# The first unit's matrix cut in halves, the second x loaded in two transfers, and one VectorE cut that reads SBUF: a batched matrix product with residual

## The reference

```python
def _L0_cond_ref(x, fwd_steps, T):
    Tb = T[fwd_steps - 1]
    return jnp.einsum('bij,bjk->bik', Tb, x)

def reference(x, itok_B_1_98, L0_cond_T):
    return x + _L0_cond_ref(x, itok_B_1_98, L0_cond_T)
```

## Time and profile before

| | before |
|---|---|
| median of 3 runs | 104.38 us (104.21 to 104.92) |
| the profiled execution's own time | 104.17 us |
| its span, first to last instruction | 102.4 us |
| TensorE busy | 95.8 us (94%) |
| VectorE busy | 86.9 us (85%) |
| GpSimd busy | 72.7 us (71%) |
| ScalarE busy | 66.0 us (64%) |
| mean rate of the transfers | 247 GB/s |

### The profile page before, as it was taken

The page is one execution under the profiler, slowest core; times in us unless marked ns, Lnnn a source line. Parts: engine busy times, 40 slices in busy tenths (PEclk is TensorE's granted clock), DMA queues, the critical chain, the costliest instruction groups (busy, mean ns, idle before and its releaser), DMA issues.

```text
span 102.4 us, 1799 instructions
## 1 busy us (share of the span) xinstructions
PE 95.8 (94%) x440; PEld 79.8 (78%) x440; DVE 86.9 (85%) x99; ACT 66.0 (64%) x86; POOL 72.7 (71%) x38
## 2 busy tenths in 40 slices
PE   4968999999999999999999999999999999999950
PEld 4957888868888888888888888888888888888840
DVE  0074798999999999999999999999999999993250
ACT  0765699659578685858585859587786858462100
POOL 2000548999989799897979797979798996918100
PEclk9999999999999999999999999999999999999999
DMA  1899999994899889897998489999899730405064
GB/s 48 299 223 407 343 219 214 378 310 125 355 319 293 273 261 326 273 315 207 353 336 274 98 284 352 294 349 255 266 304 323 226 147 19 189 3 205 0 276 134
DMA packets 20604, 25.28 MB, mean 247 GB/s; under 512 B 2290, under 2 KB 16882, under 8 KB 19698
## 3 DMA queue, kind: packets, MB, share of 16 engines
q10 hardware_dynamic: 3602, 15.34, 40.4%
q1 hardware_dynamic: 16992, 9.84, 36.7%
HBM read 16.78 MB, written 8.39 MB: 246 GB/s over the span
## 4 chain that ended last, share of the span: by engine, by line
PE 89%; DMA 5%; SPq 2%; DVE 0%; issue 0%
PE same L409 29%; PE same L420 28%; PE diff L431 28%; DMA T_sb<-T 5%; PE turned L397 2%; SPq L160 1%; PE same L388 1%; PE diff L441 1%; PE same L441 0%; SPq L146 0%; DVE out_sb L374 0%
## 5 line engine op out<-in xcount | busy, mean ns | idle before, releaser
L280 POOL TENSOR_TENSOR xL<-x_sb,xH 128x1024 fp32r<-128x1024 f32 x14 | 33.8, 2414 | 9.2 <-ACT xH L197 9.2
L293 POOL TENSOR_TENSOR TD_r<-TH_r,TL 128x1024 fp32r<-128x1024 f32 x14 | 33.8, 2415 | 2.5 <-issue 2.5
L409 PE MATMUL same<-xH,TH_r 128*128 128x512 f32 x128 | 34.5, 391 | 0.0
L420 PE MATMUL same<-xL,TL 128*128 128x512 f32 x128 | 34.4, 391 | 0.0
L431 PE MATMUL diff<-xD,TD_r 128*128 128x512 f32 x124 | 33.2, 390 | 0.1
L224 ACT ACTIVATE diff<-same 128x512 f32<-128x512 f32 x31 | 18.0, 582 | 22.2 <-PE same L420 22.2
L330 DVE STREAM_TRANSPOSE turned<-T_sb 128x512 f32<-128x512 f32 x28 | 29.1, 1085 | 0.0
L409 PEld LDWEIGHTS same<-xH,TH_r 128*128 128x128 f32 x128 | 23.9, 188 | 5.1 <-ACT TH_r L209 0.2
L420 PEld LDWEIGHTS same<-xL,TL 128*128 128x128 f32 x128 | 23.9, 188 | 4.9
L431 PEld LDWEIGHTS diff<-xD,TD_r 128*128 128x128 f32 x124 | 23.2, 188 | 5.3 <-issue 0.5
L350 DVE TENSOR_TENSOR out_sb<-x_sb,diff 128x512 f32<-128x512 f32 x31 | 21.0, 678 | 4.7 <-PE diff L431 4.7
(11 more groups left out here) (20 smaller groups left out, 18.7 us busy)
## 6 DMA issues: line engine op xcount, KB each, us to landing
out<-out_sb ACTq DMA_DIRECT2D x15, 512.0 KB, 5.1
T_sb<-T SPq DMA_DIRECT2D x112, 64.0 KB, 4.3
x_sb<-x ACTq DMA_DIRECT2D x6, 1024.0 KB, 6.3
x_sb<-x SPq DMA_DIRECT2D x1, 1024.0 KB, 10.0
x_sb<-x ACTq DMA_DIRECT2D x2, 256.0 KB, 3.7
x_sb<-x ACTq DMA_DIRECT2D x1, 512.0 KB, 4.6
T_sb<-T SPq DMA_DIRECT2D x2, 256.0 KB, 5.6
T_sb<-T SPq DMA_DIRECT2D x1, 512.0 KB, 6.8
```

Source lines behind the costliest of these rows:

```text
L280: nc.gpsimd.tensor_tensor(half(xL, h), x_sb[b % X_SLOTS][:, i:i + 2], half(xH, h).bitcast(fp32), ALU.subtract).then_inc(xL_ready, 2)
L293: nc.gpsimd.tensor_tensor(TD_r[s][:], TH_r[s][:].bitcast(fp32), TL[s][:].bitcast(fp32), ALU.subtract).then_inc(TD_ready, 2)
L409: nc.tensor.matmul(same[U % 2][:], TH_r[p][:, i, j], xH[s][:, j], start=(j == 0), stop=False)
L420: done = nc.tensor.matmul(same[U % 2][:], TL[p][:, i, j], xL[s][:, j], start=False, stop=(j == N - 1))
```

## The change

Unit 0 is turned into both banks of `turned`, two blocks in each, and TH(0) and TL(0) are made in two pieces of 256 columns, one for each bank; the first two matmuls of high(0) wait for the first piece alone. Because unit 0 now lies in both banks, turn(1) waits until TL(0) is made. The three matmuls of the unit matrix behind turn(0) go ahead of it (`WARM` 10 for 7 and 3). x of batch 1 comes in two transfers of 512 KB, each with a semaphore of its own, and `cut_x_half(2)` and `cut_x_half(3)` wait for one each. xD of half 1 reads xH in SBUF, and ScalarE's copy of half 1 is left out. GpSimd's TD(1) waits for that xD.

```diff
-    WARM, REWARM = 7, 3
+    WARM = 10
...
+        first_halves = [(turned[:, 0, 0:2], slice(0, 2)), (turned[:, 1, 2:4], slice(2, 4))]
...
             load_T(sp, t, 0)
-            load_x(sp, 1)
+            load_second_x(sp, 0)
+            load_second_x(sp, 1)
             sp.wait_ge(itok_loaded, 16)
...
             def cut_x_half(h):
                 b = h // 2
-                act.wait_ge(x_loaded[b % X_SLOTS], 16 * ((b - 1) // X_SLOTS + 1))
+                if b == 1:
+                    act.wait_ge(half_x_loaded[h % 2], 16)
+                else:
+                    act.wait_ge(x_loaded[b % X_SLOTS], 16 * ((b - 2) // X_SLOTS + 1))
...
+            def cut_first_T():
+                for i, ready in enumerate((first_half_TH_ready, TH_ready)):
+                    bank, blocks = first_halves[i]
+                    if i == 0:
+                        act.wait_ge(first_half_turned, 1)
+                    else:
+                        wait_turned(act, 1)
+                    nc.scalar.activation(TH_r[0][:, 0, blocks], bank, COPY, scale=LEAN / RADIX).then_inc(ready, 1)
...
-            cut_T(0)
+            cut_first_T()
             copy_xH_half(0)
             cut_T(1)
-            copy_xH_half(1)
             seed(0)
...
             def cut_T(U):
                 pool.wait_ge(TL_ready, U + 1)
+                if U == 1:
+
+                    pool.wait_ge(xD_ready, N)
...
-                dve.wait_ge(xH_copied, 2 * h + 2)
+
+                if h != 1:
+                    dve.wait_ge(xH_copied, max(h, 1))
...
+                high = half(xH, h).bitcast(fp32) if h == 1 else xH_copy[:]
+                nc.vector.scalar_tensor_tensor(half(xD, h), half(xL, h).bitcast(fp32), -RADIX, high,
                                                ALU.mult, ALU.add).then_inc(xD_ready, 2)
...
+            def cut_first_T():
+                for i, ready in enumerate((first_half_TH_ready, TH_ready)):
+                    bank, blocks = first_halves[i]
+                    dve.wait_ge(ready, 1)
+                    cut = nc.vector.scalar_tensor_tensor(TL[0][:, 0, blocks], TH_r[0][:, 0, blocks].bitcast(fp32), -RADIX,
+                                                         bank, ALU.mult, ALU.add)
+                cut.then_inc(TL_ready, 1)
...
+            def turn_first():
+                wait_T_loaded(pe, 0)
+                rows = T_sb[0][:, 0].rearrange("p (c j) -> p j c", j=N)
+                for j in range(N):
+                    done = nc.tensor.transpose(turned[:, j // 2, j], rows[:, j], eye[:])
+                    if j == 1:
+                        done.then_inc(first_half_turned, 1)
+                done.then_inc(turned_by_pe, 1)
...
             def turn(U):
                 s, n = U // N % T_SLOTS, U % N
                 wait_T_loaded(pe, U)
-                if U >= 2:
-                    pe.wait_ge(TL_ready, U - 1)
+                pe.wait_ge(TL_ready, max(U - 1, 1))
...
-                pe.wait_ge(TH_ready, U + 1)
                 for j in range(N):
+                    if U == 0 and j < 2:
+                        pe.wait_ge(first_half_TH_ready, 1)
+                    else:
+                        pe.wait_ge(TH_ready, U + 1)
...
             warm_up()
-            turn(0)
-            rewarm(REWARM)
+            turn_first()
             multiply_high(0)
```

More of the change, by code:

```diff
@@ L69, in cond_resid @@
         first_x_loaded = [sem(f"first_x_loaded{i}") for i in range(len(FIRST_X))]
+        half_x_loaded = [sem(f"half_x_loaded{i}") for i in range(2)]
         T_loaded = [[sem(f"T_loaded{s}_{n}") for n in range(N)] for s in range(T_SLOTS)]
@@ L72, in cond_resid @@
         turned_by_dve = sem("turned_by_dve")
+        first_half_turned = sem("first_half_turned")
+        first_half_TH_ready = sem("first_half_TH_ready")
         TH_ready = sem("TH_ready")
@@ L135, in half, with load_x, load_second_x @@
             return tiles[h // 2 % X_SETS][:, 2 * (h % 2):2 * (h % 2) + 2]
-        def load_x(eng, b, tiles=slice(0, N)):
-            eng.dma_start(x_sb[b % X_SLOTS][:, tiles], x_part[b, :, tiles]).then_inc(x_loaded[b % X_SLOTS], 16)
+        def load_x(eng, b):
+            eng.dma_start(x_sb[b % X_SLOTS][:], x_part[b]).then_inc(x_loaded[b % X_SLOTS], 16)
+        def load_second_x(eng, i):
+            eng.dma_start(x_sb[1][:, 2 * i:2 * i + 2], x_part[1, :, 2 * i:2 * i + 2]).then_inc(half_x_loaded[i], 16)
         def load_T(eng, t, b, blocks=range(N)):
@@ L202, in copy_xH_half @@
                     act.wait_ge(xD_ready, 2 * h)
-                nc.scalar.activation(xH_copy[:], half(xH, h).bitcast(fp32), COPY).then_inc(xH_copied, 2)
+                nc.scalar.activation(xH_copy[:], half(xH, h).bitcast(fp32), COPY).then_inc(xH_copied, 1)
+            def cut_first_T():
[6 more added lines that the diff above has]
+                    nc.scalar.activation(TH_r[0][:, 0, blocks], bank, COPY, scale=LEAN / RADIX).then_inc(ready, 1)
             def cut_T(U):
@@ L319, in cut_x_half @@
                     dve.wait_ge(xL_ready, 2 * h - N + 2)
-                dve.wait_ge(xH_copied, 2 * h + 2)
+                if h != 1:
+                    dve.wait_ge(xH_copied, max(h, 1))
                 if h // 2 >= X_SETS:
                     dve.wait_ge(diff_ready, (h // 2 - X_SETS + 1) * N)
-                nc.vector.scalar_tensor_tensor(half(xD, h), half(xL, h).bitcast(fp32), -RADIX, xH_copy[:],
+                high = half(xH, h).bitcast(fp32) if h == 1 else xH_copy[:]
+                nc.vector.scalar_tensor_tensor(half(xD, h), half(xL, h).bitcast(fp32), -RADIX, high,
                                                ALU.mult, ALU.add).then_inc(xD_ready, 2)
@@ L383, in warm_up @@
                         nc.tensor.matmul(diff[i][:, j * P:(j + 1) * P], eye[:], eye[:], start=(j == 0), stop=(j == N - 1))
-                rewarm(WARM)
-            def rewarm(times):
-                for _ in range(times):
+                for _ in range(WARM):
                     nc.tensor.matmul(same[1][:, 0:P], eye[:], eye[:], start=True, stop=True)
+            def turn_first():
[6 more added lines that the diff above has]
+                done.then_inc(turned_by_pe, 1)
             def turn(U):
```

## The result

| | before | changed |
|---|---|---|
| median of 22 runs each, taken side by side | 104.82 us (103.96 to 106.02) | 104.10 us (103.37 to 104.79) |
| span of the profiled execution | 102.4 us | 102.3 us |

A forecast was written before the change was run, and what follows sets the result against it. TensorE's product lines, full from 30 to 95 us, were taken to bound the kernel, so only an earlier start helps. A 0.46 us head start gives 0.45 off 104.38: 103.93 us, range 103.4 to 104.55.

The forecast's parts named there:

- The sum: At the opening's end, high(0)'s head start of 0.46 us gives 0.45 us off the whole time.
- The halves' own cost: Cutting TH(0) in two costs ScalarE some 0.14 us more, but only the first piece is on the path.
- the new wait: Turn(1)'s weight load now waits for TL(0), costing between nothing and 0.08 us; 0.01 taken.
- Passed on unaltered: TensorE's loop is full and untouched, so a shift of its start of 0.35 to 0.5 us is handed through.
- The hole stays: TensorE's 0.22 us gap ahead of diff(3), which waits for GpSimd's TD(3), remains because both paths shift alike.
- xD from SBUF: VectorE's xD of half 1 starts near 12.0 and takes 1.23 us; a length up to 2.2 us is hidden.
- x in two transfers: x's first half lands near 12.5 us, in time for xH at 14.0; unsplit, 14.34 would have allowed 0.1 us gain.
- The three matmuls moved ahead: Unit-matrix matmuls ahead of turn(0) end at 7.35, before T lets it start at 8.01; cost nothing.
- The clock: Rival: 0.23 us idle between turn(0) and high(0) leaves TensorE at half speed, losing 1.7 us; chance 0.04.

The follow-up runs named there:

- no_pool_wait: The changed kernel without GpSimd's wait, so TD(1) starts at TL(1)'s end beside VectorE's xD of half 1; ratio to before 0.9956.
- x_late: The changed kernel with x of batch 1 in one transfer, issued behind the first four pieces of T of batch 1; ratio to before 1.0105.
- no_warm: The changed kernel with WARM = 0, without the 20 unit-matrix rows behind the first 16 and ahead of turn(0); ratio to before 1.0120.
- changed_again: The changed kernel run once more with no edit; ratio to before 0.9940.

## Why the prediction was right

- *The sum.* 0.46 us from halving TH(0): 1.44 to 0.98, in eight profiles. Its parts, expected at 0.25 for two transposes and 0.21 for the shorter piece, measured 0.24 and 0.22.
- *The halves' own cost.* ScalarE's pieces take 0.66 us together from 8.95, VectorE's 0.75 (0.60 and 0.69 whole), so the pair costs ScalarE 0.06 more and not the 0.14 of the prediction, since the pieces overlap. The Trainium skill, VectorE: DVE Perf Modes, section on the TRN2 errata, which the prediction drew on there, gives its advice on tiles for instructions that read SBUF, while ScalarE's pieces read PSUM; no run here tests it for SBUF. Turn(1) starts 1.04 or 1.05 behind high(0), against 1.03: the new wait and the third matmul cost 0.02 at most.
- *Passed on unaltered.* High(0) to diff(3) and to the last product agree within 0.02 with and without the change.
- *The hole stays,* because turn(3), TH(3), xH and GpSimd's row shift with TensorE: 0.22 us, as forecast. Its price, which the prediction put at 0.22, was 0.35, since TensorE also needs more for the groups behind it.
- *xD from SBUF* took 1.22; 1.23 was forecast. For two instructions side by side the prediction had xD grow; in no_pool_wait TD(1) grew, by 0.91, and xD did not.
- *x in two transfers.* Here the prediction said too much. It rested on one execution, in which T was early: turn(0) started at 8.01, and at 9.01 and 8.77 in the two other profiles with x in one piece, while x landed at 14.34, 13.79 and 14.40. The 0.1 us to spare is T's scatter and not x's. The path is real (x_late); how often the changed kernel needs the second transfer is open.
- *The three matmuls moved ahead.* Cost nothing in nine of the ten profiles with 20 rows, where turn(0) still waited for T, and some 0.3 us in the tenth, x_late. The prediction had the rows end at 7.35, from the one profile in which they sped up earliest; they ended between 7.47 and 8.67, while T let turn(0) start from 7.89 on. What they would have cost behind turn(0), 0.19 us, I took for 0.46 in the experiment.
- *The clock.* The rival's condition, a drop behind 0.23 us of idle time, did not occur; its price, 1.7 us, was too low against the 2.07 of no_warm.

## What to carry to other kernels

When one engine is full from some instant to the end, shorten what stands before that instant: give the next engine the first part of a tile as soon as it is made, into a bank of its own, and follow each other path that starts there to the place where it meets the full engine again. Compare distances between events, not positions in the span: a first transfer that lands 0.4 us later hides a gain of the same size. An engine that causes a hole on the full one can be helped by moving its work into its own idle time, here one instruction up for 0.35 us. And work put in front to bring an engine to speed takes a time of its own, which varies: leave it room.

## What was not expected of the hardware

- turn(0), which waits for the first T of 256 KB, started between 7.89 and 9.15 us in 14 profiled executions of kernels with the same loads ahead of it (SP issued it at 2.76 to 3.12, in two at 4.52, which were not the latest). In the changed kernel alone, issued at 2.76 and 2.83, it was 8.41 and 8.86. That spread is larger than the whole effect.
- Where VectorE read two operands in SBUF beside GpSimd, GpSimd's instruction grew from 1.30 to 2.21 us and VectorE's not at all. The Trainium skill, GPSIMD Engine Reference, Key points, names the contention; the trace agrees, and shows who paid where VectorE had started first.
- After a wait of 0.22 us TensorE loses another 0.13 us over the three groups behind it (1.01, 0.92 and 0.92 us instead of 0.91). The cause is not shown.
- The granted clock reads 1.00 in the stretch of the first 16 unit-matrix rows, although they are 0.21 us apart and those behind them 0.11; the spacing is the reading to go by. The distance halves at 4.83 us in the profile of before, at 5.48 in that of the changed kernel, at 6.79 in changed_again and at 7.61 in x_late, with the same rows from 1.53 on.
